# Retention layer: q and k from high and low halves, rotation read from PSUM on VectorE, and a third summing transfer per phase

## The reference

```python
xf = group_norm(x).reshape(B, L, E)                 # B = 8 images, L = 1024 tokens, E = 256
q = heads(xf @ Wq.T)                                # 8 heads of 32
k = heads(xf @ Wk.T * SCALING)
v = heads(xf @ Wv.T)
qr = q * cos + rotate_every_two(q) * sin            # angles depend on row + column of the token
kr = k * cos + rotate_every_two(k) * sin
qk = einsum('bhqd,bhkd->bhqk', qr, kr) * mask       # mask: decay by distance, per head
den = clip(abs(qk).sum(-1), 1, 50000)
out = einsum('bhqk,bhkd->bhqd', qk / den, v)
out = gelu(layernorm_per_head(out)) @ Wo.T
x = x + out
```

## Time and profile before

| | us |
|---|---|
| median of 3 runs | 2418.18 (2417.29 to 2418.24) |
| profiled execution, its own time | 2420.93 |
| its span | 2419.1 |
| TensorE busy in the span | 2373.4 (98%) |
| VectorE | 1749.8 (72%) |
| ScalarE | 1475.5 (61%) |
| GpSimd | 1054.3 (44%) |
| mean granted clock of TensorE | 0.995 |

### The profile page before, as it was taken

The page is one execution under the profiler, slowest core; times in us unless marked ns, Lnnn a source line. Parts: engine busy times, 40 slices in busy tenths (PEclk is TensorE's granted clock), DMA queues, the critical chain, the costliest instruction groups (busy, mean ns, idle before and its releaser), DMA issues.

```text
span 2419.1 us, 38654 instructions
## 1 busy us (share of the span) xinstructions
PE 2373.4 (98%) x14870; PEld 1632.2 (67%) x14870; DVE 1749.8 (72%) x2704; ACT 1475.5 (61%) x2123; POOL 1054.3 (44%) x766
## 2 busy tenths in 40 slices
PE   8999999999999999999999899999999999999999
PEld 3444444444444444999899778888888888888887
DVE  6777778777778777677766666777777666677775
ACT  3777777777777777466565455555555554555554
POOL 4899898889898986134232101111111111001110
PEclk9999999999999999999999999999999999999999
DMA  6434444444444443255345310000000000000000
GB/s 238 97 79 105 90 111 97 105 91 112 95 105 92 88 117 91 72 82 94 67 100 82 82 52 27 27 27 27 27 27 27 27 27 27 27 27 9 18 27 18
DMA packets 89270, 165.73 MB, mean 69 GB/s; under 512 B 21488, under 2 KB 62840, under 8 KB 80768
## 3 DMA queue, kind: packets, MB, share of 16 engines
q1 hardware_dynamic: 80016, 97.21, 15.0%
q0 software_dynamic: 9072, 66.06, 13.5%
HBM read 71.93 MB, written 25.26 MB: 40 GB/s over the span
## 4 chain that ended last, share of the span: by engine, by line
PE 91%; DVE 4%; issue 2%; ACT 1%; POOL 1%; another core or an unknown queue 0%; DVEq 0%; ACTq 0%; POOLq 0%
PE scores L1775 9%; PE scores L1777 9%; PE scores L1776 9%; PE scores L429 9%; PE pairC L457 9%; PE pairD L358 5%; PE pairC L476 4%; PE pairD L407 3%; PE pairD L367 3%; PE pairC L1775 2%; PE pairC L1776 2%; PE pairC L1777 2%; PE pairD L1775 2%; PE pairD L1776 2%; PE pairD L1777 2%
## 5 line engine op out<-in xcount | busy, mean ns | idle before, releaser
L588 DVE TENSOR_TENSOR l_prod<-scores,l_window 128x1024 f32<-128x1024 f32 x512 | 603.1, 1220 | 197.4 <-PE scores L429 191.9
L781 ACT ACTIVATE l_absp<-l_prod 128x1024 f32<-128x1024 f32 x512 | 526.1, 1052 | 166.6 <-DVE l_prod L588 100.0
L2165 POOL TENSOR_TENSOR e_xnorm<-e_res,e_scale 128x1024 f32<-128x1024 f32 x16 | 39.0, 2435 | 775.6 <-DMA e_res<-t2T_scratch 775.6
L1934 ACT ACTIVATE e_r<-scores,e_bn,e_rs 128x512 f32<-128x512 f32 x256 | 197.9, 779 | 274.6 <-PE scores L1777 274.5
L910 POOL TENSOR_TENSOR l_absp<-l_absp,l_absp 128x1024 f32<-128x1024 f32 x126 | 298.2, 2388 | 10.5 <-ACT l_absp L781 10.5
L2041 DVE CAST e_h1hi<-e_r 128x512 fp32r<-128x512 f32 x256 | 146.6, 573 | 207.5 <-ACT e_r L1934 207.3
L1944 ACT ACTIVATE e_r<-scores,e_bn,e_rs 128x512 f32<-128x512 f32 x250 | 194.9, 781 | 136.9 <-PE scores L1777 135.4
L457 PE MATMUL pairC<-l_prod,l_v 128*32 128x512 f32 x2048 | 273.1, 605 | 0.0
L2068 DVE TENSOR_TENSOR e_r<-e_r,e_wbc 128x512 f32<-128x512 f32 x250 | 170.8, 690 | 85.7 <-ACT e_r L1944 85.4
L2043 DVE TENSOR_TENSOR e_h1lo<-e_r,e_h1hi 128x512 fp32r<-128x512 f32 x256 | 208.4, 814 | 8.8
L429 PEld LDWEIGHTS scores<-l_qhi,l_khi 32*128 32x128 f32 x1024 | 61.7, 181 | 218.9 <-DVE l_prod L588 134.4
(11 more groups left out here) (265 smaller groups left out, 5247.4 us busy)
## 6 DMA issues: line engine op xcount, KB each, us to landing
l_absp<-l_absp POOLq DMA_DIRECT2D x63, 1024.0 KB, 7.0
l_xo<-in_x SPq DMA_DIRECT2D x32, 256.0 KB, 2.7
x_scratch<-l_xo SPq DMA_DIRECT2D x32, 256.0 KB, 2.1
l_xa<-x_scratch SPq DMA_DIRECT2D x8, 1024.0 KB, 8.4
l_xr<-x_scratch SPq DMA_DIRECT2D x8, 1024.0 KB, 5.5
t2T_scratch<-l_xt SPq DMA_DIRECT2D x8, 1024.0 KB, 14.3
e_scale<-rows_scratch SPq DMA_DIRECT2D x16, 512.0 KB, 4.1
e_res<-t2T_scratch SPq DMA_DIRECT2D x16, 512.0 KB, 5.1
```

What stands on the lines that cost most here:

```text
L588: nc.vector.tensor_tensor(prod[2 * (S % 2) + j][:], sc[j][:], win[:, 4 * g + 2 * j:4 * g + 2 * j + 2, w0:w0 + QC], ALU.mult).then_inc(prod ...
L781: nc.scalar.activation(absp[S % ABS][j][:], prod[2 * (S % 2) + j][:], ACT.Abs).then_inc(abs_ready, 1)
L1934: nc.scalar.activation(r1[:, m, :], p1[m], ACT.Relu, bias=bn_[0][1][:, m, n:n + 1], scale=rs[0][:, m, n:n + 1]).then_inc(r1_ready, 1)
```

## The change

**Projections.** q and k are projected as three single-pass products for each half of the contraction (high x high, low x high, high x low) and no longer as one plain float32 product: six products of 128x512 in place of two. For that the weights are split once at the start (ScalarE rounds, GpSimd subtracts; the scaling of k goes into its weight there), and every normalised x is split too: ScalarE rounds it (x_high, four times an image), GpSimd subtracts (x_low); for the first image VectorE subtracts (first_x_low).

**Rotation.** The copy of the projection by ScalarE is gone. VectorE shuffles from PSUM and makes the cosine product from PSUM too (cosine): for q behind step 2 (behind step 1 in a phase with group statistics), for k behind step 4, where the shuffle moves as well. GpSimd keeps the sine product and the add. The tables of sine and cosine shrink from 1024 to 64 columns, since the angle depends on row + column; they are read with an overlapping pattern (turn).

**Sums.** Five buffers for absolute values, not six (the space goes to the high half of x). The pair (4,5) is summed by a third accumulating DMA, GpSimd adds only (6,7). The unit (0,1) is summed behind step 5 now, (2,3) behind 6, and (4,5) together with (6,7) behind step 1 of the next phase.

**Side tasks.** v is projected in two halves, in steps 5 and 6, and taken by ScalarE in step 7. Statistics of x stand at steps 0, 6, 7 and 0 of the next phase; residual adds one step earlier (step 5).

Core of the diff:

```diff
-    row(56 * K, ("l0_absp4", 8 * K), ("l0_khi1", 4 * K), ("l0_klo1", 4 * K), ("l0_absp5", 8 * K))
+    row(56 * K, ("l0_absp4", 8 * K), ("l0_khi1", 4 * K), ("l0_klo1", 4 * K), ("l0_xhi", 8 * K))
...
-    ABS = 6
+    ABS = 5
     def by_dma(P):
-        return (0, 2) if P < PHASES - 1 else (0,)
+        return (0, 2, 4) if P < PHASES - 1 else (0,)
     def by_pool(P):
-        return (4, 6) if P < PHASES - 1 else (2,)
+        return (6,) if P < PHASES - 1 else (2,)
...
-        return ((6, (0, 1)), (6, (2, 3)), (7, (4, 5)), (9, (6, 7)))
+        return ((5, (0, 1)), (6, (2, 3)), (9, (4, 5)), (9, (6, 7)))
...
+    def turn(table, c):
+        whole = table[:]
+        return bass.AP(whole.tensor, whole.offset + CROWS * c, [whole.ap[0], [1, CROWS], [1, 32]])
...
             elif before[0] == "k":
-                pe.wait_ge(t1_ready, prep_k(before[1]) + 1)
+                pe.wait_ge(shuffled, prep_k(before[1]) + 1)
+                pe.wait_ge(cos_ready, prep_k(before[1]) + 1)
...
-        def project(w, g, c, parts, to=pA, done=a_ready):
+        def project(high, low, g, c, parts, to=pA, done=a_ready):
             for k in parts:
-                mm = nc.tensor.matmul(to[:], w[:, k, 128 * g:128 * g + 128], xn[:, k, QC * c:QC * c + QC],
-                                      start=(k == 0), stop=(k == 1))
+                for n, (w, x) in enumerate(((high, xhi), (low, xhi), (high, xlo))):
+                    mm = nc.tensor.matmul(to[:], w[:, k, 128 * g:128 * g + 128], x[:, k, QC * c:QC * c + QC],
+                                          start=(k == 0 and n == 0), stop=(k == 1 and n == 2))
...
-        pe.wait_ge(first_xn, 2)
-        project(wk, 0, 0, (0, 1))
+        pe.wait_ge(w_lo, 2)
+        pe.wait_ge(xlo_ready, 2)
+        project(wkhi, wklo, 0, 0, (0, 1))
...
-            if kt == 5 and has_kv(P):
-                if part == 0:
+            if kt in (5, 6) and part == 0 and has_kv(P):
+                if kt == 5:
                     a_free(("v", P))
-                project_v(G % 2, half, (part,))
+                project_v(G % 2, half, (kt - 5,))
...
-        def shuffle(n):
-            dve.wait_ge(t1_ready, n + 1)
+        def shuffle(n, a):
+            if n > 1:
+                dve.wait_ge(lo_ready, n - 1)
+            dve.wait_ge(a_ready, a + 1)
             dve.sem_inc(waited, 1)
-            nc.vector.stream_shuffle(t2[n % 2][:], t1[n % 2][:], [i ^ 1 for i in range(32)]).then_inc(shuffled, 1)
+            nc.vector.stream_shuffle(t2[n % 2][:], pA[:], [i ^ 1 for i in range(32)]).then_inc(shuffled, 1)
+
+        def cosine(n, c):
+            nc.vector.tensor_tensor(rows(t1[n % 2][:]), rows(pA[:]), turn(cos_sb, c), ALU.mult).then_inc(cos_ready, 1)
...
             if kt == 1 and has_q(P):
-                shuffle(prep_q(P))
+                shuffle(prep_q(P), a_order["q", P])
+            if kt == (1 if has_gn(P) else 2) and has_q(P):
+                cosine(prep_q(P), (P + 1) % 2)
...
-            if kt == 5 and has_kv(P):
-                shuffle(prep_k(P))
+            if kt == 4 and has_kv(P):
+                shuffle(prep_k(P), a_order["k", P])
+                cosine(prep_k(P), P % 2)
...
-            if kt == 1 and has_q(P):
-                take(prep_q(P), a_order["q", P], 1.0)
...
-            if kt == 4 and has_kv(P):
-                take(prep_k(P), a_order["k", P], SCALING)
-            if kt == 6 and has_kv(P):
+            if kt == 7 and has_kv(P):
                 v_take(a_order["v", P], (P // 2 + 1) % 2, P % 2)
...
+            if P % 4 > 1 and P // 4 + 1 < B:
+                x_low(P // 4 + 1, P % 4 - 2)
```

More of the change, by code:

```diff
@@ L695, in vector @@
         first_normalise()
+        first_x_low()
         centre_values()
@@ L812, in first_take @@
         def first_take(n):
[L814 removed]
+            bank, ready, count = ((pA, a_ready, 3), (pB, first_made, 1), (den, first_made, 2))[n]
             act.wait_ge(ready, count)
[L816 removed]
+            nc.scalar.activation(first_t1[n], bank[:], ACT.Copy).then_inc(first_taken, 1)
         def first_v(half):
@@ L898, in low, with x_low @@
             nc.gpsimd.tensor_tensor(low, t1[n % 2][:], high.bitcast(F32), ALU.subtract).then_inc(lo_ready, 1)
+        def x_low(b, half):
+            cut = slice(QC * half, QC * half + QC)
+            for k in range(2):
+                pool.wait_ge(high_made, NHIGH + 4 * b + 2 * half + k + 1)
+                nc.gpsimd.tensor_tensor(xlo[:, k, cut], xn[:, k, cut], xhi[:, k, cut].bitcast(F32),
+                                        ALU.subtract).then_inc(xlo_ready, 1)
         def group_rstd(b):
```

133 lines of the change are left out of this document (84 added, 49 removed).

## The result

The changed kernel takes 2437.33 us (median of 4 runs, 2436.25 to 2438.66) against 2418.21 for the kernel before beside it: a ratio of 1.0074, 95% interval 1.0061 to 1.0087. It is slower by 18 us by the ratio and 19 by the medians, where 4.6 us less was forecast, and it lies above the predicted range of 2406 to 2424. The profiled execution took 2438.4 us, its span is 2436.6.

A forecast was written before the change was run, and what follows sets the result against it. It took TensorE to bound the layer, with a floor of 3.41 us per step. Phases 4 to 29 −7.0, 1 to 3 0, 0 −1.2, 30 and 31 +1.6, head +2.0: −4.6, giving 2413.6 us, range 2406 to 2424.

The forecast's parts named there:

- (a): q and k projections in steps 0 and 3: 1.36 us instead of 1.91, −1.10 us per phase.
- (b): Sum of (4,5) moved from step 7 to step 1 of the next phase: net +0.85 us per phase.
- floor step: Step with too little TensorE work: two VectorE products and the refill keep it at 3.41 us, so less work saves nothing.
- (c): v in two halves in steps 5 and 6, sum of (0,1) at step 5: cost 0.
- (d): VectorE's cosine products from PSUM: cost 0, but up to +0.3 us each in phases 0 to 3.
- (e): ScalarE's and GpSimd's changed loads in the retention layer: neither is in the chain of waits, cost 0.
- (f): Summing transfers, 7.0 us each, with five buffers and a third transfer: all land in time, cost 0.
- (g): Head before the first products: splits and normalisations delay the first projection; +2.0 us, bounds 0 to +5.
- Rival 1: No floor in the phases, so the projections' full gain counts: 2388 us; chance 5%.
- Rival 2: ScalarE late in step 2, delaying the denominator copy TensorE waits for: 2428 us if 1 us late; chance 12%.
- Rival 3: Added idle time at the new floor step lowers TensorE's clock in one phase in three: +18, 2432 us; chance 3%.
- Rival 4: Head or last two phases cost 3 to 5 us more than taken: 2417 to 2419 us, no change; chance 15%.

The follow-up runs named there:

- e4: The changed kernel with q and k projected by two plain float32 products each again: 2458.59 us, ratio 1.0155 to the kernel before.
- e11: The changed kernel with each q and k projection cut in two, three products ahead of the step's value products and three behind: 2458.18 us, ratio 1.0160.
- e6: The changed kernel with four more unread TensorE products in the pause before its first projection: 2439.97 us, ratio 1.0059.
- e3: The kernel before with only the sum of (4,5) moved from behind step 7 to behind step 1 of the next phase: 2444.51 us.
- e5: On top of e2, v projected whole in step 5 and the sum of (0,1) back behind step 6: 2427.69 us, ratio 1.0009.
- e8: The changed kernel with the cosine product of k made twice on VectorE in step 4: 2444.65 us, ratio 1.0085.
- e1: The changed kernel with the sum of (4,5) back behind step 7 and the third transfer kept: 2462.10 us, ratio 1.0168.
- e2: The changed kernel with pair (4,5) added by GpSimd again and its sum back behind step 7: 2414.22 us, ratio 0.9967.
- e9: On top of e2, the first three projections plain and the first low halves of x made by GpSimd after the normalisations: 2411.18 us, ratio 0.9966.

## Why the prediction was wrong

- **(a) failed in size.** This is the step that turned the sign. "6 x 0.227 = 1.36" is the spacing inside a run of equal products, taken from a run without edges, while the 1.91 from which it was subtracted came from the chain, with its edges. In its place a projection takes 1.59, the gain is 0.33 instead of 0.55 (e4), and e11 shows that the missing part stands at the changes of shape. Like with like gives nearly the same in the head, where three stand in a row: 5.26 / 3 = 1.75 plain, 4.17 / 3 = 1.39 from halves (e6), 0.36. The miss is 0.45 us per phase, about 12 us in phases 4 to 29.
- **(b) was right** to 0.01 us (e3). A sum moved from one step to another costs 0.86 without a product more, since a microsecond that leaves a floor step gains nothing: this mechanism decides the kernel.
- **(c) failed in size.** "0" is 0.2 us per phase, 5 us: v in halves has one group more, with its two edges (2 x 1.09 against 1.98; 28.46 against 28.66 in e5). The same oversight as (a).
- **(a) and (c) together** turn −0.27 per phase into +0.38, and +0.39 was measured. For the phases no other cause is needed.
- **(d), (e), (f) held.** VectorE has room (e8), ScalarE and GpSimd do not enter the chain, the third transfer is in time for step 1. But (f) was thought through only for the place the change chose: e1 shows that in three phases of four it would have been in time for step 7 too, and e2 that it was not needed. Its 7.0 us was a median besides; once an image a third transfer takes 12 to 13.6 us, and only the slack to step 1 hides that. GpSimd's 150 us less came out at 158, but the terms named for it add up to more, about 172 with cosines of 1.58 and 1.29.
- **(g) failed in size.** +2.0 became +4.8, inside the bounds given (0 to +5). Of the 2.8 missed, about 1.3 is a slower start of the unread products (in large part chance, as said), 1.0 the normalisations beside GpSimd, 2.2 the projections (5.81 us where 5.26 − 1.65 = 3.61 was put in: 1.6 of it the clock, as e6 shows, the rest the size of (a)); against it, 0.8 less of waiting between the splits and a reserve of 0.9 for pauses and the clock that the sum already held.
- **Phases 0 to 3** were put at −1.2 and took +1.1. Phase 0 took 0.7 more and not 1.2 less; at full clock throughout it is 0.4 shorter (28.10 in e6 against 28.54 in e3). Phases 1 to 3 took 0.4 more, where the same sum with the measured prices of (a) and (c), and 0.3 per phase for VectorE, gives 2; which of its terms is too large there, no run shows. **Phases 30 and 31**, +1.6, measured +1.5.
- **The rivals.** Rival 1 (no floor) is out: the moved sum costs its full 0.86 (e3). Rival 2 (ScalarE late) is out: TensorE waited for ScalarE twice, 1.3 us. Rival 3 was priced in the phases, where the clock stayed at 1.00 from phase 1 to 29; it came in the head and in phase 0. Rival 4 is half right, with 2.8 us. No rival held what happened, because all took the price of the projections from one row.

With the right prices, 1.59 and 2 x 1.09, the same sum gives +0.38 x 26 = 9.9 in phases 4 to 29, where 10.2 was measured: a slower kernel without the head's miss. The range was too narrow for a reason that can be named: it held ±0.1 us per phase for everything, while the one number on which the gain rested came from another place of the program.

## What to carry to other kernels

Price a group of products with its edges, not by the spacing inside a long run: where neighbours use the array in another shape, each change cost a tenth of a microsecond on either side here, so cutting a group in two is not free. And subtract like from like: a price with edges from a price with edges. Before relieving an engine, look whether it stands in the chain of waits, and what the relief forces elsewhere: here a transfer took work off GpSimd, which nobody waited for, and pushed a sum from a step with slack into one without. A mean over phases can hide one bad phase in four (e1), so list them one by one. The pieces of a change can pull in opposite directions; the halves are worth about 20 us, the third transfer with its later sum costs 23 to 26, and only taking them apart showed a version that beats both kernels.

## What the runs showed of the hardware

Some operations of VectorE from SBUF to SBUF take two to three times as long while GpSimd works on SBUF, others do not. VectorE in e9, then GpSimd:

```profile
16.70 0.74 DVE L702 STREAM_SHUFFLE l_t<-l_t 128x512 f32<-128x512 f32 x1
...
18.14 1.75 DVE L708 TENSOR_TENSOR l_t<-l_t,l_cos 128x512 f32<-128x512 f32 x1
...
21.60 1.38 DVE L713 CAST l_khi<-l_t 128x512 fp32r<-128x512 f32 x1
...
25.94 0.69 DVE L708 TENSOR_TENSOR l_tA<-l_tA,l_cos 128x512 f32<-128x512 f32 x1
...
27.46 0.43 DVE L713 CAST l_qhi<-l_tA 128x512 fp32r<-128x512 f32 x1
...
15.12 5.90 POOL L1002 TENSOR_TENSOR l_xlo<-l_xn,l_xhi 128x512 fp32r<-128x512 f32 x4 [2.09 <-ACT l_xhi L859]
```

The same product takes 1.75 us in the first place and 0.69 in the second, the same cast 1.38 and 0.43. The shuffle, beside GpSimd too, keeps its 0.74. The Trainium skill (SBUF — State Buffer, section SBUF: two separate sides) says that the two engines share one port pair as an exclusive lock, for VectorE's operations with two SBUF inputs or in a two-port mode; the rows agree. VectorE's products from PSUM keep their length in the phases, 1219 ns as before 1220, with GpSimd busy for 86 of 120 us.
